# Experts' rows added up in DRAM: one accumulating row a token, eight loads, and an earlier weighting

## The reference, cut to what matters

```python
topk_scores, topk_experts = jax.lax.top_k(probs, TOP_K)            # TOP_K = 2
cap = max(int(CAP_FACTOR * (T * TOP_K / E)), MIN_CAP)              # 1280
for e in range(E):                                                 # E = 8
    ...
    x_e = x_flat[idx]
    y_e = _ffn(x_e, W1[e], b1[e], W2[e], b2[e])                    # gelu(x w1 + b1) w2 + b2
    w = jnp.where(valid, w_tok[idx], 0.0)
    y_flat = y_flat.at[idx].add(y_e * w[:, None])
    y_flat = jnp.where(overflow[:, None], y_fb, y_flat)
```

## Time and profile before

| | |
|---|---|
| median of 3 runs | 1362.24 us (1358.11 to 1369.48) |
| the profiled execution's own time | 1360.32 us |
| its span in the profile | 1358.5 us |
| TensorE busy in the span | 1162.2 us (86%) |
| VectorE | 1043.0 us (77%) |
| ScalarE | 888.3 us (65%) |
| GpSimd | 858.8 us (63%) |
| DMA queues, share of 16 engines | 7.9% (SP's), 1.9% (GpSimd's) |

### The profile page before, as it was taken

How to read it: one execution, slowest core, us unless ns; L and a number is a source line. 1 busy time by engine, 2 the same in 40 slices (tenths; PEclk the granted TensorE clock), 3 DMA queues, 4 the chain that set the end, 5 groups by cost and what they waited for, 6 DMA issues and landing times. The chain is left out here.

```text
span 1358.5 us, 26536 instructions
## 1 busy us (share of the span) xinstructions
PE 1162.2 (86%) x7852; PEld 784.8 (58%) x7852; DVE 1043.0 (77%) x2672; ACT 888.3 (65%) x2317; POOL 858.8 (63%) x798
## 2 busy tenths in 40 slices
PE   7789999648679993896799999988969999999797
PEld 4344454335468882342577676765646777777465
DVE  6699999769859993564788788856658888887564
ACT  5534444236346560575799898977659989898663
POOL 0366656047716665315888787876568888888663
PEclk9899999769879996798999999999989999999999
DMA  4520000033212214200000000000000000000002
GB/s 134 215 67 0 1 1 1 1 88 108 65 71 71 73 55 144 67 0 24 1 2 2 2 1 2 1 1 1 0 25 2 2 2 0 1 0 2 1 1 62
DMA packets 35033, 44.08 MB, mean 32 GB/s; under 512 B 5620, under 2 KB 24977, under 8 KB 34912
## 3 DMA queue, kind: packets, MB, share of 16 engines
q1 hardware_dynamic: 30304, 34.27, 7.9%
q0 software_dynamic: 4608, 8.47, 1.9%
HBM read 22.65 MB, written 21.12 MB: 32 GB/s over the span
## 5 line engine op out<-in xcount | busy, mean ns | idle before, releaser
L2156 DVE TENSOR_TENSOR R<-bank,tab 128x1024 f32<-128x1024 f32 x128 | 155.8, 1224 | 68.9 <-ACT sq L2066 67.7
L2100 ACT ACTIVATE W<-W,nm 128x128 f32<-128x128 f32 x512 | 199.0, 396 | 0.4
L1854 POOL TENSOR_TENSOR R<-R 128x512 f32<-128x512 f32 x128 | 161.4, 1284 | 16.1 <-DVE R L2156 16.1
L2179 DVE CUSTOM_DVE_ANT_0 W<-bank,mask_q,rn 128x128 f32<-128x128 f32 x512 | 147.5, 344 | 17.3 <-PE bank L1975 13.8
L1869 POOL TENSOR_TENSOR W<-W,rden 128x512 f32<-128x512 f32 x128 | 132.6, 1042 | 40.3 <-DVE rden L2186 35.0
L1364 POOL DMA_INDIRECT expert_rows<-Yt,xin x80 | 82.4, 1030 | 67.6 <-DVE Yt L1337 48.3
L1064 POOL DMA_INDIRECT expert_slots<-tok_rows,dst x64 | 67.9, 1060 | 65.1 <-ACT tok_rows L1088 44.0
L2100 ACT ACTIVATION_READ_ACCUMULATOR W<-W,nm 128x1 f32 x512 | 99.7, 195 | 0.0
L2084 ACT ACTIVATE QK<-bank 128x512 f32<-128x512 f32 x128 | 75.3, 588 | 34.8 <-PE bank L1950 33.9
L2000 PE MATMUL bank<-PT,VA 128*64 128x128 f32 (+1 forms) x1024 | 85.4, 260 | 4.2 <-ACT PT L2108 3.3
L1975 PE MATMUL bank<-QK 64*64 64x128 f32 x2048 | 85.8, 283 | 3.4 <-DVE nm L2179 3.0
(11 more groups left out here) (358 smaller groups left out, 3506.1 us busy)
## 6 DMA issues: line engine op xcount, KB each, us to landing
expert_slots<-empty SPq DMA_DIRECT2D x8, 650.0 KB, 6.3
xin<-expert_slots SPq DMA_DIRECT2D x8, 650.0 KB
expert_rows<-empty SPq DMA_DIRECT2D x8, 512.0 KB, 6.7
pair_rows<-expert_rows SPq DMA_DIRECT2D x16, 256.0 KB, 4.2
expert_raw<-w1e_dram SPq DMA_DIRECT2D x9, 256.0 KB, 2.9
expert_raw<-w2e_dram SPq DMA_DIRECT2D x9, 256.0 KB, 3.5
tok<-x_dram SPq DMA_DIRECT2D x8, 256.0 KB, 5.2
out_dram<-tok_out SPq DMA_DIRECT2D x8, 256.0 KB, 2.7
```

The lines of the kernel that those rows point to most:

```text
L1854: nc.gpsimd.tensor_tensor(halves[:, :, 0, :, z, :], halves[:, :, 0, :, z, :], halves[:, :, 1, :, 1 - z, :], ALU.add).then_inc(summed, 1)
L2100: m = nc.scalar.activation(x, x, ACT.Exp, scale=-1.0, bias=nm[:, p % RING, j:j + 1], accum_out=den[:, p % RING, j:j + 1])
L2156: nc.vector.tensor_tensor(R[:, i, qk, :, :].rearrange("p c (h d) -> p c h d", d=DH), x, y.to_broadcast([P, 2, HEADS, DH]), ALU.mult).then_ ...
L2179: m = nc.vector.tensor_tensor_reduce(W[:, p % RING, j * P:(j + 1) * P], ps[BS[i]][:, cols], k.const["mask_q"][:, cols], rn[:, par, 2 * s + ...
```

## The change

Three edits that belong together, and one move.

1. expert_rows has one row a token (4096 rows). tokid is the token's number for both choices. The table's clears are four transfers instead of eight.
2. The sends to expert_rows add to what stands in DRAM (compute_op add). Since two accumulating writes to one row may not overlap, GpSimd waits, before part a of each expert but the first, until all sends of the experts before it have landed.
3. Eight loads (load_sum), all issued before the experts' block ends, one a chunk with a buffer each, instead of sixteen. The pair sums on GpSimd and VectorE are gone; TensorE waits for the loads themselves.
4. In steps from the third on, weighted stands behind the second of the four splits instead of behind the fourth. The last two iterations, which have no splits, are as before.

```diff
-N_CLEAR = NE + 2 * T // (8 * P)
+N_CLEAR = NE + T // (8 * P)
...
-        self.ys = nc.dram_tensor("expert_rows", (2 * T, P), F32, kind="Internal").ap()
+        self.ys = nc.dram_tensor("expert_rows", (T, P), F32, kind="Internal").ap()
...
-                for q in range(2 * T // (8 * P)):
+                for q in range(T // (8 * P)):
...
-def load_pair(k, sp, Y, y_in, q):
-    for c in range(2):
-        rows = k.ys[c * T + q * CH:c * T + (q + 1) * CH, :].rearrange("(p t) w -> p (t w)", p=P)
-        sp.dma_start(Y[:, q % NPB, c, :], rows).then_inc(y_in[q], 16)
+def load_sum(k, sp, Y, y_in, q):
+    rows = k.ys[q * CH:(q + 1) * CH, :].rearrange("(p t) w -> p (t w)", p=P)
+    sp.dma_start(Y[:, q, :], rows).then_inc(y_in[q], 16)
...
-            for q in range(NPB):
-                load_pair(k, sp, Y, y_in, q)
+            for q in range(NCH):
+                load_sum(k, sp, Y, y_in, q)
...
-                if i > 1:
+                        if i > 1 and j == 1:
+                            weighted(i - 2)
+                elif i > 1:
                     weighted(i - 2)
...
             for s, (e, t0, nt) in enumerate(STEPS):
+                if t0 == 0 and e > 0:
+                    for i, (_, n) in enumerate(EPARTS):
+                        pool.wait_ge(sent[i], 16 * n * e)
                 pool.wait_ge(yt_r, s + 1)
                 for t in range(nt):
                     ids = xin[e % 3][:, t0 + t, P + 1:P + 2].bitcast(mybir.dt.uint32)
                     nc.gpsimd.indirect_dma_start(k.ys[:, :], bass.IndirectOffsetOnAxis(ap=ids, axis=0), Yt[:, s % 3, t, :],
-                                                 None, bounds_check=2 * T - 1, oob_is_err=False).then_inc(sent[s % 3], 16)
+                                                 None, bounds_check=T - 1, oob_is_err=False,
+                                                 compute_op=ALU.add).then_inc(sent[s % 3], 16)
...
-            for q in range(NPB, NCH):
-                sp.wait_ge(turned, q - NPB + 1)
-                load_pair(k, sp, Y, y_in, q)
...
-            for q in range(0, NCH, 2):
-                first, second = (Y[:, q % NPB, c, :] for c in range(2))
-                pool.wait_ge(y_in[q], 32)
-                nc.gpsimd.tensor_tensor(first, first, second, ALU.add).then_inc(summed_pool, 1)
...
-                pe.wait_ge((summed_pool, summed_dve)[q % 2], q // 2 + 1)
+                pe.wait_ge(y_in[q], 16)
...
-            for q in range(0, NCH, 2):
-                add_pair(q + 1)
-                add_residual(q)
-                add_residual(q + 1)
...
-    c["tokid"] = (np.arange(2)[None, :, None] * T + np.arange(NT)[None, None, :] * P + np.arange(P)[:, None, None]).astype(np.uint32)
+    c["tokid"] = (np.zeros(2, int)[None, :, None] + np.arange(NT)[None, None, :] * P + np.arange(P)[:, None, None]).astype(np.uint32)
```

More of the change, by code:

```diff
@@ L913, in load_slots @@
         slots.x_in[e % 3], 16)
-NPB = 5
-def load_pair(k, sp, Y, y_in, q):
-    for c in range(2):
-        rows = k.ys[c * T + q * CH:c * T + (q + 1) * CH, :].rearrange("(p t) w -> p (t w)", p=P)
-        sp.dma_start(Y[:, q % NPB, c, :], rows).then_inc(y_in[q], 16)
+def load_sum(k, sp, Y, y_in, q):
+    rows = k.ys[q * CH:(q + 1) * CH, :].rearrange("(p t) w -> p (t w)", p=P)
+    sp.dma_start(Y[:, q, :], rows).then_inc(y_in[q], 16)
 UNITS = 5
@@ L1371, in combine @@
         sem = lambda n: ctx.enter_context(nc.semaphore(n))
-        summed_pool, summed_dve, turned, resid = map(sem, ("pair_sum_pool", "pair_sum_dve", "pair_turned", "resid_e"))
+        turned, resid = map(sem, ("sum_turned", "resid_e"))
         k.last_spent = resid.num
         block = ctx.enter_context(nc.Block())
-        @block.sync
-        def _(sp):
-            for q in range(NPB, NCH):
-                sp.wait_ge(turned, q - NPB + 1)
-                load_pair(k, sp, Y, y_in, q)
         @block.gpsimd
@@ L1392, in _ @@
             for q in range(NCH):
-                pe.wait_ge((summed_pool, summed_dve)[q % 2], q // 2 + 1)
+                pe.wait_ge(y_in[q], 16)
                 for t in range(4):
-                    m = nc.tensor.transpose(ps[q][:, t * P:(t + 1) * P], Y[:, q % NPB, 0, t * P:(t + 1) * P], k.const["ident"][:])
+                    m = nc.tensor.transpose(ps[q][:, t * P:(t + 1) * P], Y[:, q, t * P:(t + 1) * P], k.const["ident"][:])
                 m.then_inc(turned, 1)
@@ L1399, in _ @@
         def _(dve):
-            def add_pair(q):
-                first, second = (Y[:, q % NPB, c, :] for c in range(2))
-                dve.wait_ge(y_in[q], 32)
-                nc.vector.tensor_tensor(first, first, second, ALU.add).then_inc(summed_dve, 1)
-            def add_residual(q):
+            for q in range(NCH):
                 x = k.XT[:, chunk(q)].rearrange("d (p t) -> d t p", t=4)
@@ L1420, in experts @@
         slots = slot_buffers(k, big)
-        y_in = [big.enter_context(k.nc.semaphore(f"pair_in{q}")) for q in range(NCH)]
+        y_in = [big.enter_context(k.nc.semaphore(f"sum_in{q}")) for q in range(NCH)]
         routing(k, w, wide, slots)
-        Y = k.sb("pair_rows", [P, NPB, 2, CH], ctx=big)
+        Y = k.sb("sum_rows", [P, NCH, CH], ctx=big)
         expert_layers(k, w, wide, slots, Y, y_in)
```

## The result

| | before | changed |
|---|---|---|
| median, measured side by side | 1364.01 us (4 runs) | 1399.37 us (4 runs, 1395.94 to 1401.92) |
| ratio, 95% interval | | 1.0263 [1.0233, 1.0294] |
| profiled execution, its span | 1360.3, 1358.5 us | 1398.0, 1396.2 us |
| first send to first load of the sums | 126.3 us | 170.2 us |
| first load to the next stage's first copy | 20.3 us | 13.5 us |

The change makes the kernel 35.4 us slower, 20 us beyond the upper end of the predicted range. The loss lies before the first load, and the combining gives back more than forecast. Executions of one kernel fall into faster and slower ones; a ratio compares the faster ones alone, while a median here is that of all runs, so the two need not agree (the traces of early_close and one_block_psum are of slower executions).

What follows compares the result with a forecast made beforehand. TensorE was taken to pace the experts' stage, GpSimd's queued sends to set its end. Combining -5.2 and later landing +1.05 gave -4.1 us, so 1358 us from a 1362.2 median; range 1351 to 1379.

Steps and rivals of the forecast that it cites:

- the issue of an accumulating send: Experts' stage, GpSimd: each adding send taken at the plain send's 1.28 us, so no added cost.
- the slow form: Sends in the earlier trace at 1.47 + 0.30 = 1.77 us, taken as upper bound for issuing an adding send.
- second rival: Experts' stage: dearer issue on GpSimd, all 80 sends pay; 1387 us at 1.77; chance 0.18 (dearer issue or landing beyond 1%).
- The landing: Adding send's start to landing: 3.1 us, plain 2.2 plus 0.9 for reading rows; stage end then 1.05 us later.
- The wait for landings: GpSimd before each expert's part a: free in the steady part while a landing takes under 3.2 us.
- The earlier Yt: Experts' stage, VectorE: part a tiles 1.24 us earlier, parts b and c 2.43 us; mostly used up by the wait.
- The combining: From first load to next stage: eight loads and no pair sums, 14.7 us instead of 19.9, a gain of 5.2.

Runs made afterwards that it cites:

- early_close: weight_move with the experts' block closed after four loads instead of ten, the other twelve issued in the next block; 1408.3 us, 0.9933 of before.
- one_block_psum: one_block with the pair sums made in PSUM by TensorE products with the identity; 1405.6 us, 0.9955 of before.
- accum_alone: Kernel before with only the 80 sends to expert_rows adding instead of writing; 1392.9 us, 1.0207 of before.
- weight_move: Kernel before with only weighted moved behind the second pair of splits; 1362.54 us, 0.9989 of before.
- after_plain: Changed kernel with its sends writing instead of adding; 1356.08 us, 0.9945 of before.
- after_unmoved: Changed kernel with weighted put back behind the fourth pair of splits; 1436.7 us, 1.0237 of before.
- accum_waits: Kernel before with adding sends and the waits for the previous experts' landings; 1444.8 us, 1.0274 of before.
- accum_64: accum_alone with each send cut to the first 64 of 128 rows; median send 1403 ns.
- waits_alone: Kernel before with only the waits for the previous experts' landings added ahead of part a's sends; 1366.35 us, 1.0018 of before.
- plain_64: Kernel before with its plain sends to expert_rows cut to the first 64 of 128 rows; median send 907 ns.
- one_block: weight_move with the combining moved into the experts' block, no block end between; 1410.2 us, 1.0038 of before.
- one_block_dve: one_block with all eight pair sums on VectorE and none on GpSimd; 1398.4 us, 0.9964 of before.

## Why the prediction was wrong

**The failed step is one term: the issue of an accumulating send.** The prediction wrote: "For the issue on GpSimd I take the plain send's 1.28, since nothing in the trace speaks for more". It measured 1.55 + 0.30 = 1.85 us (accum_alone, and 127.6 us for 80 sends in the changed kernel). The upper bound of 1.77, from the slow form in the earlier trace rows, was too low as well, and the range didn't even hold that bound: it stops at d = 1.6. At d = 1.77 the formula gives a last landing at 561.5 and not at 557, so 1391 us and not 1387. The sensitivity stood in the text: the gain gone at 1.37, 1% lost at 1.55. Its second rival's formula with d = 1.85 gives 399.5 + 7 x 21.15 + 16.65 + 3.1 = 567.3 for the last landing, which with its own combining makes 1397 us, against 1399.4 measured. The last landing was at 570.3; that the sends' mean is 1.596 us and not 1.55 adds 3.7 us over 79 of them, which more than covers the 3.0 missing. The mechanism was written down, and given 0.18.

**Why it was given so little.** The argument against it was that 80 sends of 512-byte rows and 64 of 520-byte rows take the same, "which looks like a fixed cost". For plain sends that is nearly true: 64 rows instead of 128 take only 0.07 us off. But both groups are plain sends, and equal cost within one kind says nothing about another kind. The fixed part itself grew, from 0.84 to 1.26 us by the two points.

**The landing** was right in its number: 3.1 forecast, 3.2 measured in the median, with plain 2.2. In its reason it was partly luck. The forecast gave all of its 0.9 us to reading the rows in DRAM, and chose them between two bounds far apart. Of the 1.0 us measured, 0.57 are GpSimd's longer record, the very term put at nothing, and some 0.4 lie behind the record's end.

**The wait for landings.** Right as long as its premise holds: with plain sends GpSimd waits 12.6 us and the stage loses 1.9. The formula's slack was reckoned at 1.28 us a send. At 1.85 the condition 9 x 1.85 + 4.5 < 16.12 fails, the expert costs 21.15 us by the formula (21.5 measured, 150.3 us from the first expert's first send to the last expert's at 550.44, over seven), and the wait costs 14.5. The forecast priced wait and issue as two terms, though the first is free only while the second is small; the rival's formula had them together.

**The earlier Yt.** The first send comes 1.2 us earlier in weight_move (1.24 forecast), and the kernel doesn't get slower. Right as far as the runs can tell.

**The combining.** -5.2 forecast, -6.8 measured: the right sign, partly for a wrong reason. Of the 1.6 us more, 0.6 come from the residual sums (0.99 each, not 1.06) and 1.0 from the block's opening, 4.1 us after the first load and not 5.1. The forecast took before's 1.33 us from SP's last load to VectorE's start for the price of an opening. But in before SP wasn't what the opening waited for: with plain sends it follows GpSimd's last send (early_close), after 6.9 us on TensorE in after_plain and 7.25 on VectorE elsewhere. In the changed kernel SP's eighth load is

```profile
573.54 0.43 SPq L918 DMA_DIRECT2D sum_rows<-expert_rows  x1
```

and TensorE comes in 0.44 us after its end, as it does in after_unmoved. accum_alone has ten loads; its tenth, and GpSimd's first sum:

```profile
559.24 0.53 SPq L922 DMA_DIRECT2D pair_rows<-expert_rows  x1
...
560.68 2.95 POOL L1389 TENSOR_TENSOR pair_rows<-pair_rows 128x512 f32<-128x512 f32 x2 [7.38 <-ACTq L1371]
```

GpSimd comes in 0.91 us after the tenth load, in accum_waits and accum_64 0.90 and 0.91; with plain sends it is 1.20 to 4.35. So in the five kernels with accumulating sends the opening fits SP's last load, not GpSimd's last send, from whose end it is 5.7 us with eight loads and 7.3 with ten. The number of loads does count there, as the forecast had it, at 0.44 us behind them in place of 1.33.

**What remains open.** Why a block in which GpSimd has sent rows opens the next one some 7 us after GpSimd's last work, if the sends are plain; it was found in before, weight_move, waits_alone, plain_64, early_close, after_plain and, behind a plain sum, in one_block, and was covered in one_block_dve and one_block_psum. No run takes it apart. Behind accumulating sends GpSimd holds the opening up by 5.7 us at most; why by less than behind plain ones isn't known. And whether GpSimd's 0.57 us go into writing the descriptors of 144 packets or into a setup of their kind was not separated beyond the two sizes.

## What to carry to other kernels

Price a new kind of an instruction by itself before the sum is made, above all one that an engine issues eighty times; a flat cost over sizes of the old kind is no evidence for the new one. A wait is free only at a stated spacing of what it stands among, so put both into one formula, and see from which price the next engine becomes the pacer: here 0.09 us a send stood between gain and loss. Where a sum can be made by an idle VectorE from plain rows, in 0.7 us a chunk of 512 tokens, it is cheaper here than an accumulating send at 0.57 us more for every 128 rows.

## What the runs showed of the hardware

- An accumulating indirect send of 128 rows of 512 bytes holds GpSimd 1.55 us (shortest 1546 ns) against 0.97 plain, both with 0.30 us to the next; it lands 3.2 us after its start against 2.2, and makes 144 packets against 32.
- At 64 rows it is 1.40 against 0.91 us, 80 packets against 32: the packets follow the rows, the time on GpSimd hardly does. It lands 0.3 to 0.4 us sooner than at 128.
- Behind the end of GpSimd's last plain send of a block, the next block opened for VectorE 7.25 us later (before, weight_move, waits_alone, plain_64, early_close), whether SP had ten or four loads to issue, and it costs nothing when another engine works that long (one_block_dve: 0.4 us behind VectorE).
- Behind accumulating sends it opened with SP's last load: 0.44 us after it for TensorE (the changed kernel and after_unmoved), 0.90 to 0.91 for GpSimd (accum_alone, accum_waits, accum_64).
- The granted clock of TensorE, 1.00 from 400 to 513 before, is 0.93 in the same stretch of the changed kernel, where TensorE has gaps (100.97 of 113 us busy).
